# Attention scores as bands of 160 keys, probabilities transposed in 32x32 blocks by VectorE, values replicated for 32x64 tiles

## The reference

```python
q = rmsnorm((x @ wq.T).reshape(B, T, 16, 64), q_norm_w)      # x is the layer-normed input
k = rmsnorm((x @ wk.T).reshape(B, T, 4, 64), k_norm_w)
v = (x @ wv.T).reshape(B, T, 4, 64)                          # 4 heads of q share one of k and v
scores = jnp.einsum('bqhd,bkhd->bhqk', q, k) / 8
mask = (i >= j) & (i - j < 128)                              # a window of 128 keys
attn = softmax(where(mask, scores, -inf))
x = x + einsum('bhqk,bkhd->bqhd', attn, v) @ wo.T
gate = softmax(xn @ gate_w.T)                                # xn is x, layer-normed again
x = x + xn @ weight.T + (1/16) * sum_e gate_e * lora_V_e (lora_U_e xn)
```

## Time and profile before

| what | value |
|---|---|
| median of 3 runs (lowest, highest) | 2342.57 us (2341.37, 2344.53) |
| profiled execution | 2341.73 us, its span 2340.0 us |
| TensorE busy | 2308.2 us, 99% |
| VectorE busy | 2098.9 us, 90% |
| ScalarE busy | 2053.1 us, 88% |
| GpSimd busy | 1110.6 us, 47% |
| granted TensorE clock, mean | 0.997 |
| DMA | 44.30 MB, mean 19 GB/s |

### The profile page before, as it was taken

One profiled execution on the slowest core, in us unless ns is written; L12 is line 12 of the kernel. 1 busy time (PEld: TensorE's weight loads), 2 busy tenths in 40 slices (PEclk: granted clock), 3 DMA queues, 4 the chain that ended last, 5 costly groups with the idle time before them and its releaser, 6 DMA issues.

```text
span 2340.0 us, 118291 instructions
## 1 busy us (share of the span) xinstructions
PE 2308.2 (99%) x49424; PEld 1977.6 (85%) x49424; DVE 2098.9 (90%) x6767; ACT 2053.1 (88%) x7175; POOL 1110.6 (47%) x1516
## 2 busy tenths in 40 slices
PE   7999999999999999999999999999999999999998
PEld 4888888888888888888888888888888888888886
DVE  7999899999998998999999989998999899899986
ACT  6888888898888888888988889888889888898886
POOL 3444444544454445445444554454455444544442
PEclk9999999999999999999999999999999999999999
DMA  2000000000000000000000000000000000000000
GB/s 73 12 21 17 17 16 21 17 17 17 21 17 17 19 19 17 17 21 17 16 17 21 17 17 17 21 17 17 17 21 17 17 20 17 17 17 21 17 10 14
DMA packets 39919, 44.30 MB, mean 19 GB/s; under 512 B 4448, under 2 KB 38624, under 8 KB 39392
## 3 DMA queue, kind: packets, MB, share of 16 engines
q1 hardware_dynamic: 39392, 36.73, 5.1%
HBM read 19.93 MB, written 16.78 MB: 16 GB/s over the span
## 4 chain that ended last, share of the span: by engine, by line
PE 75%; ACT 14%; DVE 9%; issue 1%; POOL 0%; DMA 0%; SPq 0%; DVEq 0%
PE ps_a L684 9%; PE ps_scores L729 9%; PE ps_y L751 7%; PE ps_d L678 5%; ACT probs L348 5%; PE ps_d L680 5%; PE ps_d L679 5%; PE ps_y L764 5%; PE ps_c L684 4%; PE ps_y L781 4%; PE ps_b L678 3%; PE ps_b L680 3%; PE ps_b L679 3%; PE ps_b L684 2%; ACT qT L333 2%; PE ps_a L680 2%
## 5 line engine op out<-in xcount | busy, mean ns | idle before, releaser
L348 ACT ACTIVATE probs<-merged,neg_max 128x128 f32<-128x128 f32 x2048 | 801.0, 396 | 91.0 <-DVE neg_max L522 86.9
L243 POOL TENSOR_TENSOR q_r<-q_ve,minus_half 128x8 f32<-128x8 f32 x256 | 420.5, 1643 | 270.7 <-DVE q_ve L495 264.1
L265 POOL TENSOR_SCALAR_AFFINE_SELECT pT_other<-pT 128x256 f32<-128x256 f32 x384 | 160.3, 417 | 567.3 <-ACT pT L356 567.1
L348 ACT ACTIVATION_READ_ACCUMULATOR probs<-merged,neg_max 128x1 f32 x2048 | 397.3, 194 | 0.0
L729 PE MATMUL ps_scores<-kT,qT 64*32 64x160 f32 (+4 forms) x16384 | 377.7, 281 | 4.4 <-DVE neg_max L515 3.1
L533 DVE TENSOR_TENSOR probs<-probs,rden 128x512 f32<-128x512 f32 x512 | 353.2, 690 | 8.5
L356 ACT ACTIVATE pT<-ps_a 128x512 f32<-128x512 f32 x512 | 307.3, 600 | 11.3 <-PE ps_a L684 1.0
L684 PE MATMUL ps_a<-ident,probs 128*128 128x128 f32 x2048 | 314.5, 276 | 0.3 <-DVE q_n L501 0.2
L678 PE MATMUL ps_d<-wo_h,yT_h 128*128 128x256 f32 x1024 | 309.4, 302 | 0.7 <-ACT qT L333 0.7
L248 POOL TENSOR_TENSOR h_rstd<-h_ve,minus_half 128x1 f32<-128x1 f32 x128 | 118.4, 925 | 371.0 <-DVE h_ve L557 371.0
L680 PE MATMUL ps_d<-wo_l,yT_h 128*128 128x256 f32 x1024 | 288.3, 282 | 0.0
(11 more groups left out here) (119 smaller groups left out, 6139.3 us busy)
## 6 DMA issues: line engine op xcount, KB each, us to landing
xs<-x SPq DMA_DIRECT2D x128, 128.0 KB, 2.1
out<-ob SPq DMA_DIRECT2D x128, 128.0 KB, 2.1
...
w_plain<-w_o SPq DMA_DIRECT2D x8, 128.0 KB, 5.5
...
w_plain<-w_v SPq DMA_DIRECT2D x1, 128.0 KB, 5.0
nw<-norm_w SPq DMA_DIRECT2D x1, 1.0 KB, 5.1
```

The lines of the kernel that those rows point to most:

```text
L243: pool.tensor_tensor(q_r[:, T % DEEP, c], q_ve[:, T % DEEP, c], minus_half[:, 0:8], ALU.pow).then_inc(s_qr[n], 1)
L348: last = nc.scalar.activation(probs[:, r, h], merged[:, r, h], ACT.Exp, bias=neg_max[:, r, h:h + 1], scale=1.0 if slot(T) else -1.0, accum ...
```

## The change

Scores are now stored as a band. For a block n of 32 queries the 160 keys at columns 32n to 32n+160 are written to columns 0 to 160 of `ps_scores`, whatever the block, and all four heads of a group keep 160 columns through the softmax (`soft`, in place of `merged` and `probs`).

- `mask_and_max` (VectorE): one fused instruction for each head in every tile, on 160 columns, adds a mask (`mask_band`, or `mask_first` in the first tile of a sequence), writes `soft` and takes the row maximum. `own_scores`, `merge` and `maximum` are gone.
- q is no longer normalised before its transpose. ScalarE copies it out of PSUM (`copy_q`), the row maximum is multiplied by -1 and by q's factor in a small VectorE instruction (`scaled_max`), and the exponential takes q's factor as its scale operand, read from SBUF beside the bias operand. `norm_q` is gone.
- The probabilities are normalised by GpSimd for groups 0, 1 and 2 (`norm_probs`, 128x640) and by ScalarE for group 3 (`normalise`, four instructions of 160 columns), no longer by VectorE.
- The transpose of the probabilities is one VectorE instruction for each group, which turns every 32x32 block of 128x640 by itself, each staying at its place (`transpose_probs`). TensorE's transposes of the probabilities, `store_pT` and `select` are gone.
- After such a transpose the 32 keys of block j lie on the partitions of the 32 queries of block n. So each partition group of 32 needs the values of every key block: SyncE starts 16 DMAs for each tile (`replicate`), which copy each of the 4 blocks of 32 values to each of the 4 partition groups of `v_rep`. The values are stored once (`v_own`); `v_diff` is gone.
- `attend` multiplies by the values for all heads of a tile at once, in 32x64 tiles of the array: 80 products (40 in the first tile of a sequence), into `ps_y`, which now has four banks. These four banks are also `ps_a` to `ps_d`; `ps_e` and `ps_f` hold one half of q and the output projection, and the feed-forward part. y is written in two pieces of 512 columns in place of four of 256.
- The order in every `step` is new.

The core of the diff:

```diff
+            def replicate(T):
+                if live(T):
+                    sp.wait_ge(s_v, done(T))
+                    if live(T - 3):
+                        sp.wait_ge(s_pv, done(T - 3))
+                    for j in range(BLOCKS):
+                        for n in range(BLOCKS):
+                            sp.dma_start(v_rep[QUARTER * n:QUARTER * n + QUARTER, (BLOCKS * T + j) % (DEEP * BLOCKS)].rearrange("p g d -> p (g d)"),
+                                         v_own[QUARTER * j:QUARTER * j + QUARTER, T % 2]).then_inc(s_vr[T % WIDE], 16)
...
+            def norm_probs(T, g):
                 if live(T):
                     r = ring(T, g)
                     pool.wait_ge(s_rden, groups(T, g))
+                    pool.tensor_tensor(soft[:, r], soft[:, r], rden[:, r].unsqueeze(2).to_broadcast([P, REP, SPAN]), ALU.mult).then_inc(s_pn, 1)
...
+            def copy_q(T, n):
+                if live(T):
+                    act.wait_ge(s_q[n], done(T))
+                    nc.scalar.activation(q_raw[:, T % 2, 8 * n:8 * n + 8].rearrange("p (c e) d -> p e c d", e=2),
+                                         ps_q[n][:].rearrange("p (e c d) -> p e c d", e=2, d=HD), ACT.Copy).then_inc(s_qc[n], 1)
...
             def exps(T, g, heads):
                 if live(T):
                     r = ring(T, g)
+                    act.wait_ge(s_max, groups(T, g))
                     for h in heads:
-                        last = nc.scalar.activation(probs[:, r, h], merged[:, r, h], ACT.Exp, bias=neg_max[:, r, h:h + 1], scale=1.0 if slot(T) else -1.0,
+                        head = 8 * (g // 2) + 4 * (h // 2) + 2 * (g % 2) + h % 2
+                        last = nc.scalar.activation(soft[:, r, h], soft[:, r, h], ACT.Exp, bias=neg_max[:, r, h:h + 1], scale=q_r[:, T % DEEP, head:head + 1],
                                                     accum_out=den[:, r, h:h + 1])
...
+            def normalise(T, g):
+                if live(T):
+                    r = ring(T, g)
+                    act.wait_ge(s_rden, groups(T, g))
+                    for h in range(REP):
+                        last = nc.scalar.activation(soft[:, r, h], soft[:, r, h], ACT.Copy, scale=rden[:, r, h:h + 1])
+                    last.then_inc(s_pna, 1)
...
+            def mask_and_max(T, g):
+                if live(T):
+                    r = ring(T, g)
+                    wait(dve, s_pt, groups(T, g) - RING)
+                    dve.wait_ge(s_s, groups(T, g))
...
+                    for h in range(REP):
+                        last = nc.vector.tensor_tensor_reduce(soft[:, r, h], ps_scores[:, h, 0:SPAN], mask_band[:] if slot(T) else mask_first[:], 1.0, LOWEST,
+                                                              ALU.add, ALU.max, accum_out=raw_max[:, r, h:h + 1])
+                    last.then_inc(s_mm, 1)
+
+            def scaled_max(T, g):
+                if live(T):
+                    r, n = ring(T, g), g // 2
+                    dve.wait_ge(s_mm, groups(T, g))
                     dve.wait_ge(s_qr[n], done(T))
+                    rms = q_r[:, T % DEEP, 8 * n:8 * n + 8].rearrange("p (e a c) -> p a e c", e=2, a=2)[:, g % 2]
+                    nc.vector.scalar_tensor_tensor(neg_max[:, r].rearrange("p (e c) -> p e c", e=2), raw_max[:, r].rearrange("p (e c) -> p e c", e=2), -1.0, rms,
+                                                   ALU.mult, ALU.mult).then_inc(s_max, 1)
...
+            def transpose_probs(T, g):
...
+                    if live(T - 1):
+                        dve.wait_ge(s_pv, done(T - 1))
+                    nc.vector.transpose(pT[:, g // 2, :, g % 2].rearrange("p e c k -> p e (c k)"), soft[:, ring(T, g)].rearrange("p (e c) k -> p e (c k)", e=2)).then_inc(s_pt, 1)
...
+            def attend(T):
+
+                pe.wait_ge(s_pt, groups(T, KV_HEADS - 1))
+                pe.wait_ge(s_vr[T % WIDE], REPLICAS * (T // WIDE + 1))
+                for p in range(2):
+                    for j in range(BLOCKS + 1):
+                        for n in range(BLOCKS):
+                            first = 0 if slot(T) else BLOCKS - n
+                            if j < first:
+                                continue
+                            rows, keys = slice(QUARTER * n, QUARTER * n + QUARTER), (BLOCKS * (T - 1) + n + j) % (DEEP * BLOCKS)
+                            for half in range(2):
+                                last = nc.tensor.matmul(ps_y[HD * half:HD * half + HD, n, P * p:P * p + P], v_rep[rows, keys, 2 * p + half],
+                                                        pT[rows, p, half, :, :, QUARTER * j:QUARTER * j + QUARTER], start=j == first, stop=j == BLOCKS, skip_group_check=True)
+                last.then_inc(s_pv, 1)
```

491 lines of the change are left out of this document (182 added, 309 removed).

## The result

The changed kernel takes 2243.68 us (median of 4 runs, 2238.83 to 2248.26), the kernel before 2342.12 (4 runs, 2341.37 to 2344.53): a ratio of 0.9578, with a 95% interval of 0.9555 to 0.9600. The forecast was 2255. The profiled execution has a span of 2246.4 us and a mean clock of 0.991.

A forecast was written before the change was run, and what follows sets the result against it. VectorE was taken as the bound after the change, TensorE before: 14.9 own work plus 2.3 held, 17.2 us a tile; 128 x 17.2 = 2202 plus 52 filling and draining, 2254, so 2255 us; 8 in 10 range 2065 to 2410.

The forecast's parts named there:

- The sum: Whole kernel: 128 tiles at VectorE's 17.2 us, 2202, plus 52 of filling and draining, span 2254, time 2255 us.
- VectorE, own work, 14.9 us: VectorE's instructions without the holds: 16.26 us a tile less 9.87 gone plus 8.5 added, 14.9.
- VectorE, held, 2.3 us: VectorE's small instructions with two SBUF inputs wait behind GpSimd's streaming multiplications, a loss of 2.3 us a tile.
- TensorE, 15.2 us: TensorE's work a tile: 17.92 less 1.76 (transposes) and 3.21 (value products) plus 2.2 (attention), 15.2 us, at worst 17.2.
- rival 2: Weights of 64 columns pace TensorE's attention at 0.029 us a pass: 18.4 us a tile, 2409 us; chance 0.13.
- ScalarE, 15.4 us: ScalarE's work a tile: 15.96 less 3.8 gone plus 3.3 added, 15.4 us, below VectorE.
- What hides the rest: GpSimd stays under 13.4 us a tile; the 16 DMAs, about 2.1 us each, are wanted over 20 us later.
- Rival 1: VectorE's holding by GpSimd mostly hidden or small; three engines within 0.5 us, 16.1 us a tile, 2115 us; chance 0.25.
- rival 3: VectorE's transposes run at half rate, 1.4 us each: 19.7 us a tile, 2575 us; chance 0.08.
- The signs named: TensorE busy below 90%, VectorE leading the chain, transposes near 0.8 us, GpSimd multiplications near 1.6, attend passes at 0.015.

The follow-up runs named there:

- e2_norm4: The changed kernel in its own order, with GpSimd's multiplication of the probabilities cut to 4 of 640 columns: 2179.61 us, ratio 0.9300 to the kernel before.
- e1_order: The changed kernel with VectorE's small instructions with two SBUF inputs moved away from GpSimd's multiplications: 2180.03 us, ratio 0.9296 to the kernel before.
- e10_order_half: e1_order with the attention of groups 2 and 3 left out, 80 passes a tile in place of 160: 1996.75 us, one execution.
- e4_nocopy: The changed kernel with SyncE's copies of the values made for the first four tiles only, later waits for them dropped: 2226.96 us, ratio 0.9502.
- e11_padded_good: e1_order with two buffers of pT and 20 more semaphore instructions in each turn of TensorE: 2115.93 us, ratio 0.9038 to the kernel before.

## Why the prediction was right, point by point

**The sum.** The forecast was tiles of 17.2 us and 52 of filling and draining, 2254; measured are 17.21 and 43.5, 2246.4. The tile agrees to 0.01 us, and this is in part luck: VectorE is 0.9 shorter than forecast and a loss of 0.9 that I didn't know of takes its place. Without that loss and with the rest as it is, the same sum would have given 16.3 us a tile and some 2130 us, and the forecast of 2255 would have been 6% too high. The whole difference in the span, 8 us, is the filling.

**VectorE, own work, 14.9 us.** Too high: 16.3 busy less 2.0 held is 14.3, and e2_norm4 has 14.6 (the printed durations overlap a little, so the first is the rougher). The durations were right: a transpose took 0.75 from start to start (1007.27 to 1008.02), with 0.73 taken and 1.4 as the upper end; a fused mask 0.24 for 0.25. So it is the subtraction that kept too much. A part of it can be seen: `q_ve` and `k_ve` were held by v_diff before, at a mean of 224 and 214 ns in that trace, and take 156 and 133 now, 0.2 us a tile that I had left in the 16.26. The rest, 0.1 to 0.4, I can't name.

**VectorE, held, 2.3 us.** Measured is 2.0 by durations, `scaled_max` 0.235 over its free 0.158, four times, 0.9; `gate` 0.78; `g_negmax` 0.31; and 1.7 by VectorE's busy time with and without the holds (e2_norm4). The mechanism, and the three instructions that stand behind a release of GpSimd, were as argued from the order and from the earlier trace rows. Of the sizes, `gate` at 0.8 for 1.2, `g_negmax` at 0.3 for 0.5 and `scaled_max` at 0.9 for 1.2 are each too high, and a part of it is that GpSimd's multiplication takes 1.25 us and not 1.6; `q_ve` and `k_ve` are never held. Powers don't hold here either: the two `scaled_max` that began inside one took 0.16, and in e1_order 128 did and took 0.153. The Trainium skill, page "SBUF — State Buffer", section "Who interferes with whom", makes no difference between a multiplication and a power: any GpSimd instruction that reads SBUF contends with a VectorE instruction with two inputs there. The streaming multiplications agree with that (126 of 126 `gate`), the powers don't.

**TensorE, 15.2 us.** It was too low, as e1_order shows, where the chain is TensorE's: tiles without a stop take (15.55 + 3 x 16.1) / 4 = 16.0. Attention is right: 2.48 us by the rows above for 2.35 + 0.16, and rival 2, weights that set the pace, would have shown 4.3. In the first tile of a sequence it takes 1.9 (e1_order; 2.5 with waits in the changed kernel) where I had half, 0.15 a tile as a mean. The larger part is the scores, which I said "stay at 0.54 a group": they now take 0.70 (1024.52 to 1025.22), 0.60 in a first tile. Before, most of them stood between two value products of the same small tiles; now each group has 128x128 products or the attention's 32x64 tiles on either side. The difference, 0.16, is what I had read there as the price of entering such a stretch, and had charged once a tile: together 0.5 us. By the traces it is the change of tile form that costs, and at the end of the group: from the last pass of a group to the next instruction it is 0.09 us in the kernel before, where other 64x32 products follow, and 0.23 in e1_order, before 128x128 products and before the 32x64 attention alike.

**ScalarE, 15.4 us.** 15.23 by e10_order_half. An exponential takes 0.51 from start to start for 0.45 (too low), a normalising instruction 0.32 for 0.38 (too high). Together they add 0.7 to my sum, and it came out 0.2 too high all the same: work that I had left as it was got cheaper, such as the copies that write `xT_h` and `hT_h` and the square of k, which went from 0.33 to 0.38 us to 0.27 each. So the closeness of this sum is luck too. ScalarE is below VectorE, as forecast.

**What hides the rest.** No wait for the copies is in the list, but that they cost nothing while the cover holds was wrong as far as e4_nocopy tells: it finds 0.7%, with the caveat given there.

**Rivals.** Rival 1 (no holds, 2115) names its condition, a `scaled_max` near 0.2 us; it is 0.39. With the holds away, in e1_order and e2_norm4, the kernel takes 2180 and not 2115, since TensorE's 16.0 and its stops are then in the way. e11_padded_good comes to 2116 with both away, but by TensorE at 16.1 a tile and not by three engines near 14.9: that the number is rival 1's is chance. Rival 2 and rival 3 fail on 0.0143 us a pass (160 passes in 2.27 us undisturbed) and 0.75 us a transpose.

**The signs named.** VectorE does not lead the chain alone (35% against 37%), and TensorE is busy for 94%, not under 90%. These two missed. The first leads to TensorE, by its own work and by the stops; the second is my 15.2, since 16.0 of 17.2 us is 93% without any stop. L485 and L466, named among the held, were free, and L272 took 1.25 us for 1.6. The transposes, the attention's passes and the means of L505, L563 and L573 came as named.

**The stops, 0.9 us a tile, not in the prediction.** The step that misses them is the one that took TensorE's time as a sum of passes. The profile before could not show them: the longest such stretch there is a group's value products and scores. The term was put at nothing because I did not count instructions, only time.

**What stays open.** When a packet is asked for, which no run varied. The trace of the changed kernel bears on it: for block ends inside the attention of a full tile, up to 226 instructions behind its start, the packet starts 2.0 us or more before the end is reached, and for those from 234 on, almost always, 0.2 to 1.6 us before it. That would fit a request some 230 instructions ahead, so that it falls into the attention in the second case, but this is a reading and not shown. Open too are the unnamed part of VectorE's own work above, what the 0.9 us a tile hold besides the gaps, and by what way the edit of e4_nocopy shortens the stops.
